# A two-layer transformer kernel on one Trainium2 core: gates spread by PE, the first attention's output projection and the router computed transposed

## The reference, cut to what matters

```
x = x + 0.5 * _L0_ffn_ref(ln(x), Wr, br, W1, b1, W2, b2)    # MOE0_A
x = x + _L0_attn_ref(ln(x), wq, bq, wk, bk, wv, bv, wo, bo)  # ATT0
x = x + 0.5 * _L0_ffn_ref(ln(x), ...)                        # MOE0_B, same weights
x = x + 0.5 * _L1_ffn_ref(ln(x), gate_w, expert_w, expert_b) # MOE1_A
x = x + _L1_attn_ref(ln(x), Wq, Wk, Wv, Wo)                  # ATT1
x = x + 0.5 * _L1_ffn_ref(ln(x), gate_w, ...)                # MOE1_B
```

## Time and profile before

| | |
|---|---|
| three runs | 699.38, 703.26, 709.02 us; median 703.26 |
| the profiled execution | 708.19 us, of which its span is 706.2 us |
| TensorE clock granted, mean over the span | 0.964 of 2.4 GHz |

### The profile page before, as it was taken

One profiled execution on the slowest core, in us unless ns is written; L12 is line 12 of the kernel. 1 busy time (PEld: TensorE's weight loads), 2 busy tenths in 40 slices (PEclk: granted clock), 3 DMA queues, 4 the chain that ended last, 5 costly groups with the idle time before them and its releaser, 6 DMA issues.

```text
span 706.2 us, 7645 instructions
## 1 busy us (share of the span) xinstructions
PE 655.9 (93%) x2395; PEld 415.2 (59%) x2395; DVE 465.5 (66%) x1059; ACT 432.3 (61%) x922; POOL 181.3 (26%) x132
## 2 busy tenths in 40 slices
PE   3699998999999999999999999999999989889974
PEld 2456565556656555676576666666566645556552
DVE  5677467643447964737769957858886757386752
ACT  4345456444447554697486478657379524968685
POOL 3120000100002111144042025214014432676565
PEclk9899999999999999999999999989999998989998
DMA  8782621063333107612223222200613000000000
GB/s 244 162 164 67 112 63 38 22 122 65 102 75 60 59 3 132 96 26 65 42 61 62 65 55 60 60 1 11 111 60 61 0 1 0 1 15 1 16 16 15
DMA packets 27026, 42.22 MB, mean 60 GB/s; under 512 B 1689, under 2 KB 8938, under 8 KB 26986
## 3 DMA queue, kind: packets, MB, share of 16 engines
q1 hardware_dynamic: 26986, 41.74, 27.1%
HBM read 40.42 MB, written 1.31 MB: 59 GB/s over the span
## 4 chain that ended last, share of the span: by engine, by line
PE 67%; ACT 12%; DVE 9%; SPq 5%; DMA 4%; issue 2%; POOL 1%; POOLq 0%; ACTq 0%; DVEq 0%
PE py L1122 26%; PE ph L900 7%; PE ph L902 7%; PE ph L901 7%; ACT stage L547 5%; ACT bc L547 4%; DMA bc<-comb_rows 3%; PE ps L1030 2%; SPq L358 2%; DVE stage L756 2%; PE ps L1031 2%; PE ps L1032 2%; SPq L331 1%; PE ps L1004 1%; PE ps L1005 1%
## 5 line engine op out<-in xcount | busy, mean ns | idle before, releaser
L596 ACT ACTIVATE g<-ph,b1col 128x512 f32<-128x512 f32 x256 | 172.7, 695 | 153.3 <-PE ph L902 120.1
L1122 PE MATMUL py<-hw,w2s 128*128 128x512 f32 x512 | 250.0, 612 | 1.9 <-DVE hw L859 1.9
L859 DVE TENSOR_TENSOR hw<-g,bc 128x1024 f32<-128x1024 f32 x128 | 166.8, 1310 | 110.4 <-ACT g L596 93.2
L1122 PEld LDWEIGHTS py<-hw,w2s 128*128 128x128 f32 x512 | 97.2, 194 | 77.7 <-issue 64.4
L900 PE MATMUL ph<-xbh,w1h 128*128 128x512 f32 x256 | 137.4, 537 | 0.0
L388 POOL TENSOR_TENSOR rstd<-vare,mhalf 128x4 f32<-128x4 f32 x24 | 35.4, 1477 | 358.3 <-DVE vare L672 358.1
L547 ACT ACTIVATE stage<-ps,comb 128x128 f32<-128x128 f32 x384 | 106.3, 564 | 10.4 <-PE ps L1032 10.2
L902 PE MATMUL ph<-xbh,w1l 128*128 128x512 f32 x256 | 102.7, 401 | 0.0
L901 PE MATMUL ph<-xbl,w1h 128*128 128x512 f32 x256 | 102.6, 401 | 0.0
L448 POOL TENSOR_TENSOR stage<-stage 128x1024 f32<-128x1024 f32 x24 | 57.4, 2393 | 68.4 <-ACT stage L547 68.4
L900 PEld LDWEIGHTS ph<-xbh,w1h 128*128 128x128 f32 x256 | 49.7, 194 | 30.8 <-issue 22.6
(11 more groups left out here) (199 smaller groups left out, 865.0 us busy)
## 6 DMA issues: line engine op xcount, KB each, us to landing
bc<-comb_rows SPq DMA_DIRECT2D x31, 1024.0 KB, 8.8
stage<-in_L_ffn_W_dram SPq DMA_DIRECT2D x4, 512.0 KB, 6.5
X<-in_L_attn_x_dram SPq DMA_DIRECT2D x4, 256.0 KB, 3.1
bc<-comb_rows SPq DMA_DIRECT2D x4, 256.0 KB, 5.5
out_dram<-X SPq DMA_DIRECT2D x4, 256.0 KB, 2.3
comb_rows<-combT SPq DMA_DIRECT2D x8, 32.0 KB, 5.3
side<-in_L_attn_wq_dram SPq DMA_DIRECT2D x1, 64.0 KB
side<-in_L_attn_wk_dram SPq DMA_DIRECT2D x1, 64.0 KB
```

The lines of the kernel that those rows point to most:

```text
L596: nc.scalar.activation(g[:, s % 2, h, 0:w], ph[:, (HC * s + h) % RING_PH, 0:w], ACT.Gelu, bias=b1col[:, HC * e + h:HC * e + h + 1]).then_i ...
L859: V.tensor_tensor(hw[:, s % RING_HW, :, 0:w], g[:, s % 2, :, 0:w], bc[:, s // GQ % 2, s % GQ, 0:w].unsqueeze(1).to_broadcast([P, HC, w]), ...
L1122: ins = T.matmul(py[:, 0:cols], w2s[:, w], hw[:, s2 % RING_HW, h, 0:cols], start=e2 == 0 and h == 0, stop=False)
```

## The change

Five edits, and a new order of turns for all engines.

1. Router: the weights (32 columns) become stationary and the 512 tokens move, first `xbh`, then `xbl`, so the logits come out as 32 rows of 512. ACT copies them to `lgT` and adds the bias there, which now lies on partitions (`brcol`). PE turns the four tiles back. The K=1 bias matmul is gone; lo times low part is added where it was left out.
2. ATT0: one float32 matmul with `wos` stationary and `vv` moving gives the output with features on partitions; ACT's gelu takes the bias `bo`; four transposes turn it into `ps` bank 2, from where DVE adds it to `X`. PE has four steps in place of three.
3. The gates of the first three slots are spread by PE from `combT` (K=16, 512 columns, into the three `ps` banks), in the step `q0`, and DVE reads them from there. The fourth comes by one load.
4. W2 is loaded from ACT's queue, behind ACT's first copy of W1.
5. expert_w is loaded from ACT's queue, in ACT's `wt` step, behind a wait for all four parts of W1. PE's `wt` waits for the first three slots' multiplies.

In the new order of turns (not quoted: long strings of turns) the following differs. DVE: at the start `q0` and the last three parts of `w1` come ahead of the first router (before, only the second part did). PE: the second chunk's router comes one slot later, behind `q0`. For ATT0, DVE's first two steps stand together (before, one slot lay between), and the addition to X comes one to two slots earlier. The transposes and the matmuls that begin ATT1 of chunk 2 came before the end of the main stream and now come behind it.

```diff
+    PE_GATES = 3
...
@@ sync
-            sp.dma_start(w2s[:, :].rearrange("p (e c o) -> p e c o", e=E, c=HC), W2.rearrange("e (c p) o -> p e c o", p=P)).then_inc(w_in["w2"], 16)
...
                     if k == 0:
-                        for e in range(GQ):
-                            sp.dma_start(bc[:, 0, e:e + 1, 0:wide(c)], comb_dram[l // 2, e:e + 1, col(c)].partition_broadcast(P)).then_inc(bc_first[e], 16)
+                        sp.dma_start(bc[:, 0, PE_GATES:GQ, 0:wide(c)], comb_dram[l // 2, PE_GATES:GQ, col(c)].partition_broadcast(P)).then_inc(bc_first, 16)
...
-                        sp.dma_start(stage[:, 0:E * D].rearrange("p (e h) -> p e h", e=E), expert_w.rearrange("e d h -> d e h")).then_inc(w_in["we"], 16)
@@ scalar w1_
                     nc.scalar.activation(w1h[:, w1_part(i)], stage[:, w1_part(i)], ACT.Copy).then_inc(w1_high, 1)
+                    if i == 0:
+                        act.dma_start(w2s[:, :].rearrange("p (e c o) -> p e c o", e=E, c=HC), W2.rearrange("e (c p) o -> p e c o", p=P)).then_inc(w_in["w2"], 16)
@@ scalar rt
+                act.wait_ge(light["lt_ps"], nth_light("lt_ps", l, c))
+                if moe0(l):
+                    if (l, c) == MAIN[0]:
+                        act.wait_ge(w_in["router"], 32)
+                    nc.scalar.activation(lgT[:, 0:wide(c)], pl[0:2 * E, 0:wide(c)], ACT.Identity, bias=brcol[:, :]).then_inc(light["lt"], 1)
+                else:
+                    nc.scalar.activation(lgT[:, 0:wide(c)], pl[0:2 * E, 0:wide(c)], ACT.Copy).then_inc(light["lt"], 1)
                 yield
@@ scalar wt
+                act.wait_ge(w1_ready, W1_PARTS)
+                act.dma_start(stage[:, 0:E * D].rearrange("p (e h) -> p e h", e=E), expert_w.rearrange("e d h -> d e h")).then_inc(w_in["we"], 16)
@@ scalar a0_
-                nc.scalar.activation(osb, ps[:, 1, :], ACT.Gelu_apprx_tanh).then_inc(a0["o"], 1)
+                nc.scalar.activation(osb, ps[:, 1, :], ACT.Gelu_apprx_tanh, bias=bqkv[:, 3:4]).then_inc(a0["o"], 1)
@@ vector a0_
-                dve.wait_ge(a0["o"], c + 1)
-                V.tensor_tensor(X[:, col(c)], X[:, col(c)], osb, ALU.add).then_inc(a0["x"], 1)
+                dve.wait_ge(a0["ot_ps"], c + 1)
+                V.tensor_tensor(X[:, col(c)], ps[:, 2, :], X[:, col(c)], ALU.add).then_inc(a0["x"], 1)
@@ vector main
-                    if s < GQ:
-                        dve.wait_ge(bc_first[s], 16)
+                    if s < PE_GATES:
+                        dve.wait_ge(gate_ps, s + 1)
+                    elif s == PE_GATES:
+                        dve.wait_ge(bc_first, 16)
...
+                    gates = ps[:, s, 0:w] if s < PE_GATES else bc[:, s // GQ % 2, s % GQ, 0:w]
@@ tensor q0
+                l, c = MAIN[0]
+                pe.wait_ge(light["ct"], nth_light("ct", l, c))
+                for e in range(PE_GATES):
+                    T.matmul(ps[:, e, 0:wide(c)], ident[0:E, e:e + 1].to_broadcast([E, P]), combT[:, col(c)], start=True, stop=True).then_inc(gate_ps, 1)
                 yield
@@ tensor rt
-                n = ntiles(c)
-                if moe0(l):
-                    T.matmul(pl[:, 0:n * 2 * E], ones[0:1, :], brr[:, 0:n, :, :].rearrange("p t a e -> p (t a e)"), start=True, stop=False)
                 w = wr0 if moe0(l) else wr1
-                for j in range(n):
-                    t = slice(j * P, (j + 1) * P)
-                    d = pl[:, j * 2 * E:(j + 1) * 2 * E]
-                    T.matmul(d, hi[:, t], w[:, :], start=not moe0(l), stop=False)
-                    ins = T.matmul(d[:, 0:E], lo[:, t], w[:, 0:E], start=False, stop=j == n - 1 or not moe0(l))
+                T.matmul(pl[0:2 * E, 0:wide(c)], w[:, :], hi, start=True, stop=False)
+                T.matmul(pl[0:2 * E, 0:wide(c)], w[:, :], lo, start=False, stop=True).then_inc(light["lt_ps"], 1)
+                yield
+                pe.wait_ge(light["lt"], nth_light("lt", l, c))
+                for j in range(ntiles(c)):
+                    ins = T.transpose(pl[:, j * 2 * E:(j + 1) * 2 * E], lgT[:, j * P:(j + 1) * P], ident[0:2 * E, 0:2 * E])
                 ins.then_inc(light["lg_ps"], 1)
-                yield
                 yield
@@ tensor a0_
+                T.matmul(ps[:, 1, :], wos[:, :], vv, start=True, stop=True).then_inc(a0["o_ps"], 1)
+                yield
+                pe.wait_ge(a0["o"], c + 1)
                 for j in range(TPC):
-                    d = ps[:, 1, j * D:(j + 1) * D]
-                    T.matmul(d, vv[:, j * P:(j + 1) * P], wos[:, :], start=True, stop=False)
-                    ins = T.matmul(d, ones[0:1, :], bos[:, :], start=False, stop=True)
-                ins.then_inc(a0["o_ps"], 1)
+                    ins = T.transpose(ps[:, 2, j * P:(j + 1) * P], osb[:, j * P:(j + 1) * P], ident[:, :])
+                ins.then_inc(a0["ot_ps"], 1)
                 yield
@@ tensor wt
                 pe.wait_ge(w_in["l1"], 16 * 6)
+                pe.wait_ge(hw_ready, PE_GATES)
```

More of the change, by code:

```diff
@@ L87, in build_program @@
         b2s = sb("b2s", [E, D])
-        brr = sb("brr", [1, TPC, 2, E])
+        brcol = sb("brcol", [2 * E, 1])
+        lgT = sb("lgT", [2 * E, TPC * P])
         wr0 = sb("wr0", [P, 2 * E], f32r)
@@ L91, in build_program @@
         qkv0h, qkv0l = sb("qkv0h", [P, 3 * P], f32r), sb("qkv0l", [P, 3 * P], f32r)
-        bqkv = sb("bqkv", [P, 3])
+        bqkv = sb("bqkv", [P, 4])
         wos = sb("wos", [P, D])
-        bos = sb("bos", [1, D])
         qkv1h, qkv1l = sb("qkv1h", [P, 3 * P], f32r), sb("qkv1l", [P, 3 * P], f32r)
@@ L198, in build_program @@
         bc_in = [sem("bc_in0"), sem("bc_in1")]
-        bc_first = [sem(f"bc_first{e}") for e in range(GQ)]
-        light = {n: sem(n) for n in ("stat", "rstd", "xn", "xt_ps", "xh", "xl", "res", "lg_ps", "shift", "expd",
+        gate_ps = sem("gate_ps")
+        bc_first = sem("bc_first")
+        light = {n: sem(n) for n in ("stat", "rstd", "xn", "xt_ps", "xh", "xl", "res", "lt_ps", "lt", "lg_ps", "shift", "expd",
                                   "comb", "ct_ps", "ct", "yt_ps")}
         a0 = {n: sem("a0_" + n) for n in ("q_ps", "k_ps", "v_ps", "relq", "relk", "v", "minq", "mink", "expq", "expk",
-                                          "vz", "o_ps", "o", "x")}
+                                          "vz", "o_ps", "o", "ot_ps", "x")}
         f1 = {(l, late): {n: sem(f"f{l}_{late}_{n}") for n in ("y_ps", "relu_a", "relu_v", "half", "quarter", "sum", "red")}
@@ L257, in build_program @@
         STEPS = {"rt": 2, "ct": 1, "c0": 1, "a0": 3, "w1": W1_PARTS, "q0": 1, "wt": WROUNDS + 1}
-        STAGE_OF = {"lg_ps": "rt", "shift": "rt", "expd": "rt", "comb": "rt",
+        STAGE_OF = {"lt_ps": "rt", "lt": "rt", "lg_ps": "rt", "shift": "rt", "expd": "rt", "comb": "rt",
                     "ct_ps": "ct", "ct": "ct", "yt_ps": "c0"}
@@ L323, in _ @@
             sp.wait_ge(brr_zero, 1)
-            sp.dma_start(brr[:, :, 0, :], br.rearrange("(a e) -> a e", a=1).unsqueeze(1).to_broadcast([1, TPC, E])).then_inc(w_in["router"], 16)
+            sp.dma_start(brcol[0:E, :], br.rearrange("(e a) -> e a", a=1)).then_inc(w_in["router"], 16)
             for i in range(W1_PARTS):
@@ L335, in _ @@
             sp.dma_start(wos[:, :], wo).then_inc(w_in["small"], 16)
-            sp.dma_start(bos[:, :], bo.rearrange("(a p) -> a p", a=1)).then_inc(w_in["small"], 16)
+            sp.dma_start(bqkv[:, 3:4], bo.rearrange("(p a) -> p a", a=1)).then_inc(w_in["small"], 16)
             for c in range(1, NCH):
@@ L368, in _ @@
         def _(pool):
-            nc.gpsimd.memset(brr[:, :, :, :], 0.0).then_inc(brr_zero, 1)
+            nc.gpsimd.memset(brcol[:, :], 0.0).then_inc(brr_zero, 1)
             nc.gpsimd.memset(ident[:, :], 0.0).then_inc(pool_step, 1)
@@ L858, in main @@
                     w = wide(MAIN[s // E][1])
-                    V.tensor_tensor(hw[:, s % RING_HW, :, 0:w], g[:, s % 2, :, 0:w],
-                                    bc[:, s // GQ % 2, s % GQ, 0:w].unsqueeze(1).to_broadcast([P, HC, w]), ALU.mult).then_inc(hw_ready, 1)
+                    gates = ps[:, s, 0:w] if s < PE_GATES else bc[:, s // GQ % 2, s % GQ, 0:w]
+                    V.tensor_tensor(hw[:, s % RING_HW, :, 0:w], g[:, s % 2, :, 0:w], gates.unsqueeze(1).to_broadcast([P, HC, w]), ALU.mult).then_inc(hw_ready, 1)
             def wt(l, c):
```

## The result

The changed kernel takes 700.94 us (median of 12 runs, 699.45 to 703.56), the kernel before 705.32 beside it on the same chip (12 runs, 699.38 to 710.43). The ratio is 0.9943, 95% interval 0.9917 to 0.9969: about 4 us faster, clear of the noise though far under 2%, against a forecast of 3.4 us. The profiled execution took 700.25 us; its span is 698.3.

A forecast was written before the change was run, and what follows sets the result against it. PE bounds the main stream (60 to 571.8 us), ACT the tail. Terms -7.1 + 1.4 + 3.0 + 0 - 0.7 + 0 = -3.4 us take the median from 703.3 to 699.9 us; range 687 to 712.

The forecast's parts named there:

- four signs of being right: ATT0 1.3 us; router transposes 0.6 to 0.7; slot 0 at 27 to 30; main stream 3 to 7 shorter, tail equal or 2 longer.
- ATT0, -7.1: ATT0's output on PE: 2.07 us less each, four times, 0.3 each taken back; 7.1 us saved, between 3 and 9.
- The router on PE, +1.4: Router matmuls and transposes on PE: 1.21 us each against 1.33 or 0.91 before; +1.4 us, between -1 and +4.
- The router on ACT, +3.0: Router's added copies on ACT, five in the tail or relu stretches at 0.59 us: +3.0 us, between 0 and +6.
- Rival B: Trip to ACT makes routers late, at later pieces' gates and the tail's three routers: slower, 710 us; chance 0.18.
- The start, 0: Kernel start up to slot 0's multiply: slot 0 at about 28.6 us as before; 0 us, between -7 and +4.
- so they land at 20.0: At the start, the small weights that q0 waits for land between 11.2 and 21.1 us, taken as 20.0.
- Expert_b, -0.7: At the start, PE's 0.71 us wait for expert_b goes, its loads no longer behind expert_w in SP's queue: -0.7 us.
- The end of the main stream, 0: Beginning of chunk 2's ATT1 moves behind the main stream, some 3 us of PE: counted 0, between -2 and +4.
- A: At the start, small weights and W1 land early, slot 0 comes 4 us sooner at a higher clock: 693 us; chance 0.22.
- C: At the start, W2 from ACT's queue takes bandwidth from W1's later parts: slot 0 at 32, +4 us, 704; chance 0.15.
- D: At ATT0, the gain is given back: PE waits longer for DVE, clock falls longer; -7.1 becomes 0, 707 us; chance 0.07.

The follow-up runs named there:

- e2: The changed kernel with ATT0's old output (four times two matmuls, gelu without bias) put back: 711.46 us, ratio 1.0111 to the kernel before.
- e5: The kernel before in its old order, with only the new ATT0 output and one more PE turn per ATT0: 698.42 us, ratio 0.9897.
- e1: The changed kernel with the router as before the change, new order kept: 698.61 us, ratio 0.9928 to the kernel before.
- e8: The changed kernel with q0 behind the first router, X of chunk 1 loaded ahead of the small weights, and the old router: 691.43 us, ratio 0.9812.
- e7: The changed kernel with q0 behind the first router and X of chunk 1 loaded ahead of the small weights: 693.41 us, ratio 0.9840.
- e12: The changed kernel with q0 late, X of chunk 1 early, the old router, and slot 3's multiply ahead of the second router: 691.95 us, ratio 0.9838.
- e11: The changed kernel with q0 late, X of chunk 1 early, and slot 3's multiply ahead of the second router: 692.28 us, ratio 0.9840.
- e6: The changed kernel with DVE's q0 and last W1 parts moved behind or between the first router's steps: 694.93 us, ratio 0.9855.
- e4: The kernel before with only the new order of turns, all five edits undone: 712.88 us, ratio 1.0128.
- e9: The kernel before in the new order of turns, but with DVE's q0 behind the first router: 706.95 us, ratio 1.0038.
- e10: The changed kernel with W2 issued by SP again, ahead of b2 and the small weights: 702.63 us, ratio 0.9984 to the kernel before.

## Why the prediction was right, step by step

The sum was right within about a microsecond, and that was luck: the main stream won far more than I had it win, and the start and the tail lost far more. Of my own four signs of being right, only ATT0's matmul and transposes came out (1.22 us of work for 1.3). The router's transposes took 0.36 us for 0.6 to 0.7, slot 0 came at 32.5 for 27 to 30, and the main stream and the tail missed their ranges.

**ATT0, -7.1.** Right in kind, too small. At chunk 2 the 2.07 us were 1.24: the transposes took 0.36 for a forecast 0.40, but from the matmul's start to the next slot's 1.73 us passed, 0.87 more than the matmul's 0.86, where I had taken back 0.3. At chunk 1 the slot that was to cover the gelu is missing, and the place gained nothing; I had named that condition and put no price on it. What I missed altogether is the clock. The earlier trace rows already had it: the slot behind ATT0 starts with a record of 1.22 us for one matmul of 512 columns, where the earlier trace rows has four in 1.72. I used that row for its start time only. The term is -12 in the changed kernel (e2) and -7.3 in the old order (e5).

**The router on PE, +1.4.** Wrong in size and sign: 16 x 0.82 is 4.8 us less than 8 x 1.33 + 8 x 0.91. A transpose of 32 rows took 0.09 us each, not the 0.16 of one with 16 rows, nor the 0.21 that I set as the dear end. A single record behind another shape was a poor price for four in a row. Rows 4 and 5 did not bear out the rule on row groups either, as I had said they did: the operands of rows 5 have 128 rows each, so they overlap as much as those of rows 4, and they are the cheap ones; and the 32-row transposes behind matmuls with 128 rows came out at the cheap end, not the dear one.

**The router on ACT, +3.0.** The copies are 5.4 and 4.7 us of ACT, as counted. They cost nothing in the tail, where e1 is 1.3 us longer than the changed kernel and e8 1.4 longer than e7 (e12 is 4.3 shorter than e11, with other stretches at a low clock, so the tail does not decide). In the seven pieces the transposed router is ahead by 1.4 to 1.7 us in each of the three pairs (after and e1, e7 and e8, e11 and e12), once half of a 3.4 us low stretch is taken off after and e12: an estimate, and a third of the 4.8 us that PE saves over the whole span. What is left to cancel it would have to lie at the start. Rival B had the mechanism: ACT reaches the copy behind a gelu pair, PE the transposes behind half a slot, 2.6 us from the first matmul to the last transpose (40.77 to 43.40) against 1.33. It had another place. What it holds up in the changed kernel is DVE, and behind it slot 3's multiply. By the ratios, e1 against after, the edit is worth nothing: PE has 4.8 us less, DVE waits 9 us longer for logits, and that these two cancel is argued, not shown. Where the gain goes stays open.

**The start, 0.** The step that failed is "so they land at 20.0", and more so what it let pass. The small weights were ready at 21.8, `combT` at 28.45 for a forecast 26.6, and slot 0 at 32.50, outside "27 to 30 us". Of these 3.9 us the small weights are 1.8. Gate matmuls were priced at either clock, but a slot's six hidden matmuls stand ahead of them (27.48 to 30.32), and all of it ran at 1.2 GHz (5.41 us for the three gates, 30.32 to 35.73). I saw that the first router now stood behind `q0` and let it pass, because slot 0 seemed to come at the same time. e6 shows its price: 6 us.

**Expert_b, -0.7.** Right: the transpose at 53.67 follows without a wait. **The end of the main stream, 0.** Wrong: the tail is 6.9 us longer. e4 has it with no edit (+7.9), and e5 in the old order hasn't (133.9), so it is the order that moves work from the main stream to the tail. How much of that is a mere move and how much a loss was not tried alone; all parts of the order besides `q0` cost 2.7 us together (e9).

**The rivals.** A did not happen: the small weights landed at 21.8 and not early. But slot 0 can come sooner, as e6 shows: with the router free of `q0` the first piece ends 7 us sooner. C named the time of slot 0 (32) and the wrong cause. It said W2 would push W1's later parts; the third copy of W1 waited 0.42 us for its load, before and after, and the fourth for none. e10 turns its sign around: W2 from ACT's queue wins 3 us for the small weights. The Trainium skill, DMA: Bandwidth & Descriptors, section Issuing engines are not separate DMA queues, says that a second issuing engine saves issue time only. e10 agrees as far as it goes: what it costs to go back is SP's 9.78 us at one issue, and the loads that it delays. D's mechanism ran the other way: PE waits a little for DVE, and the clock stays up.

**The order** was no term of mine. I listed what it moved and priced two items of it. It costs 9 us by itself (e4), and the five edits earn 13 on top, some 12 of them ATT0's (e2).

## What to carry to other kernels

When an edit comes with a new order of work, price the order as an edit of its own, and run it alone: here one step of DVE, placed ahead of a chain that the first output needs, cost 6 us, more than the router (nothing), the gates (1.5, not clear of noise) and W2's queue (2.9) gave together by their ratios. A step that waits for a late load belongs behind everything that doesn't need it. And when small matmuls follow upon idle time, look at how long the large ones behind them take: a clock that falls there is part of the price of the small ones. Last, compare a profile with that of a kernel that should not differ in the stretch in question, before a difference there is put down to an edit.

## What I had not expected of the hardware

- The four transposes with a 32-row stationary operand took 0.36 us together, 0.09 each, right behind matmuls with 128 rows.
- A low clock came at ATT0's pair pattern (16 small records in 3.33 us, every second with one stationary row) four times in four in the kernel before, for 3.4 or 6.8 us each, and three times in four in e2, e4 and e9; with one 512-column matmul in its place, once in the changed kernel and e10, twice in e5, never in e7. PE had waited 0.48 to 1.94 us for DVE just ahead of the pattern.
- The last small load, 512 bytes, took 11.04 us from issue to landing, with 286 GB/s passing on average in that time. Issuing it 8.5 us earlier than in e10 (10.76 against 19.30) made it land 3 us earlier.
